# Computing the front of each later layer inside the last batch or chunk of the layer before it

## The chip, the cores and the metric

The program runs on one core of a Trainium2 chip. Its engines are TensorE (PE), VectorE (DVE), ScalarE (ACT), GpSimd (POOL) and SyncE (SP), which here only issues DMAs. The metric is device time in microseconds of one execution. A pair of kernels is compared by several executions of each on the same chip.

## The reference, cut to what matters

x has 16 batches of 256 tokens with 128 features. Four residual layers follow each other, each on the layer norm of x:

```python
x = x + mamba(layernorm(x))        # 16 states per channel, 256 channels, scan over 256 tokens
x = x + experts(layernorm(x))
x = x + attention(layernorm(x))    # 16 heads of 8, weights 1/(eps + distance)^2; it norms and adds its input again
x = x + experts(layernorm(x))      # the same weights as the first experts
```

The expert layer, for one token:

```python
scores = sigmoid(x @ gate_w.T)                       # 16 experts
inds = top_k(scores + expert_bias, 8)
combine = 2.826 * scores[inds] / sum(scores[inds])   # 0 for the others
y = sum_e combine[e] * w_down[e] @ (silu(w_gate[e] @ x) * (w_up[e] @ x))
y = y + shared_down @ (silu(shared_gate @ x) * (shared_up @ x))
```

All 16 experts are computed for all tokens here, and the combine weight of an expert that wasn't chosen is 0.

## The kernel before

**Stages.** x stays in SBUF (`x_sb`) for the whole program. The four layers are four calls, `mamba_layer`, `expert_layer`, `attention_layer`, `expert_layer`, each in a block of its own: all engines meet at the end of a block before any goes on to the next. Inside a block each engine has its own list of instructions, written by hand: a prologue, a first body, a hardware loop of two bodies, last bodies and an epilogue. Engines wait for each other by semaphores (`take` waits and lowers again, `Chain` makes an engine wait for its own last result). No scheduler changes this order.

**Mamba** runs by batch of 256 tokens. A body has 8 steps m (PAIRS); in each, ACT computes the decays (`L498`), POOL the inputs (`L270`), DVE the scan over time (`L643`) and its product with C (`L598`), and PE adds the states up into `m_y_ps` (`add_states`, `L374`). DVE multiplies y by the gate (`gate_y`, `L586`), PE projects out, DVE updates x (`L592`). In the block's epilogue the expert weights are converted from float32 to two float16 halves: ACT makes all the upper halves; POOL the lower halves of the down and router weights (`L312` to `L314`); DVE those of gate and up (`ew_gate_up`) in three pieces (`L666`) of 6, 6 and 5 experts, with `gate_y` and the update of the last batch between them.

**Experts** run by chunk of 512 tokens, 8 chunks. For a chunk, the front is: statistics (DVE `L1005`), norm (POOL `L838`), normalise (DVE `L1015`), transpose (PE `L861`), split into halves `x_hi` (ACT) and `x_lo` (DVE `L1020`), routing products (PE), the sigmoid by tanh (ACT), and `choose` in three parts (DVE `L1029` to `L1043`: eight linked steps from the scores to `e_comb`). PE transposes the combine weights (`L875`), ACT reads them into `e_cT`, SP stores them to DRAM (`mix`, `L805`) and loads them back spread over all partitions (`e_c_bc`, `L810`, four loads of four experts each). Then 17 steps e (16 experts and the shared one): PE computes gate and up in three matmuls each (`L885`) into one of BANKS = 3 pairs of PSUM banks `g`, `u`; ACT applies silu (`L956`), DVE multiplies by the combine weight (`e_cu`, `L1056`) and by the other half (`e_h`, `L1061`), ACT and POOL split h into halves (`L961`, `L845`), and PE multiplies by the down weights (`L892`) three steps later. A bank is free again when `e_h` has been made. The front of chunk q + 1 runs inside the body of chunk q; that of chunk 0 is the block's prologue, where the engines do nothing else, except that PE runs up to the third expert ahead. The last chunk of the layer has no front in it. x is updated at `L1066`.

**Attention** runs by batch, three batches deep. The front of a batch: statistics (DVE `L1407`), norm (POOL `L1207` to `L1213`, seven linked steps), normalise (DVE `L1418`), transpose (PE `L1271`) and projection to q, k, v, gate (PE `L1277`), read with bias (DVE `L1428`), packing and squares (POOL `L1229`), splitting q and k into halves with their norms (DVE `L1439` to `L1447`), 16 transposes (PE `L1286`) and their read (DVE `L1454`). Then 16 heads: scores (PE `L1295`), distances (DVE `L1461`), sqrt, ln and exp (ACT `L1384`, `L1388`, `L1392`), weighing of the values (PE `L1303`), division, gate, output projection, update of x (`L1497`). The prologue of the block zeroes the padded tiles (POOL), computes the front of batch 0, then the statistics and norm of batch 1.

## Time and profile before

| | us |
|---|---|
| three runs | 1593.68, 1592.61, 1593.71 |
| their median | 1593.68 |
| the profiled execution | 1592.62, of which the span is 1590.9 |
| busy PE | 1308.6 (82%) |
| busy DVE | 1273.3 (80%) |
| busy ACT | 1097.2 (69%) |
| busy POOL | 897.1 (56%) |

The shares are means over four stages with different limits: Mamba up to about 534 us, the first expert layer to 843, attention to 1278, the second expert layer to the end. They say nothing about the places where one stage hands over to the next; these are read in the timeline. The clock of TensorE has two levels, 1.2 and 2.4 GHz, and the granted clock of a stretch is given as a share of the upper one; over the whole execution it was 0.887.

### The profile page before, as it was taken

The numbers are of one execution on the slowest core, as the hardware profiler recorded it, in microseconds if no ns is written. First come the engines' busy times: TensorE is split into PE (matmuls) and PEld (weight loads), VectorE is DVE, ScalarE is ACT, GpSimd is POOL, SyncE is SP. The second block draws the span as 40 slices with busy tenths as digits, with TensorE's granted clock in tenths as the row PEclk, the third lists the DMA queues.
The fourth block names the chain that finished last, engine by engine and source line by source line (L and its number), as shares of the span: only waits on it lengthen the run. The fifth ranks groups of instructions, "written<-read, shape, count | busy, mean of one in ns | idle before, by whom it ended". The sixth has DMA issues, their size and how long they took to land. (4 is left out here: it accounts for less than half of the span.)

```text
span 1590.9 us, 21353 instructions
## 1 busy us (share of the span) xinstructions
PE 1308.6 (82%) x6384; PEld 626.4 (39%) x6384; DVE 1273.3 (80%) x2163; ACT 1097.2 (69%) x1578; POOL 897.1 (56%) x1052
## 2 busy tenths in 40 slices
PE   4688888888886499999994777778878569999998
PEld 3344444444442244444441233333333224444443
DVE  2899999999999678878864788888887357877775
ACT  4667767867866255555550899999999935555554
POOL 5898888889877365555554322322321025555555
PEclk8899999999999799999996577867766569999999
DMA  7122122122110132222220000000000022223330
GB/s 239 54 80 81 53 71 88 53 69 91 53 70 37 77 137 108 107 106 106 106 107 0 1 1 0 0 0 0 0 0 1 1 107 114 114 113 126 149 149 35
DMA packets 27923, 111.54 MB, mean 70 GB/s; under 512 B 4049, under 2 KB 9570, under 8 KB 19426
## 3 DMA queue, kind: packets, MB, share of 16 engines
q1 hardware_dynamic: 27010, 110.21, 18.5%
q10 hardware_dynamic: 864, 0.74, 0.1%
q8 instruction: 22, 0.36, 0.1%
q14 instruction: 27, 0.22, 0.0%
HBM read 108.06 MB, written 2.88 MB: 70 GB/s over the span
## 5 line engine op out<-in xcount | busy, mean ns | idle before, releaser
L845 POOL TENSOR_TENSOR e_h_lo<-e_h,e_h_hi 128x512 f16<-128x512 f32 x272 | 314.7, 1157 | 273.3 <-ACT e_h_hi L961 262.2
L270 POOL TENSOR_TENSOR m_h<-m_b_sb,m_dx 128x512 f32<-128x512 f32 x256 | 345.0, 1374 | 49.1 <-POOLq L67 40.4
L498 ACT ACTIVATE m_decay<-m_delta,mw_a_log 128x255 f32<-128x255 f32 x448 | 185.3, 461 | 119.4 <-DVEq L648 119.2
L643 DVE TENSOR_TENSOR_SCAN m_h<-m_decay,m_h 128x1024 f32<-128x1024 f32 x112 | 255.8, 2284 | 13.2 <-DVEq L60 7.5
L1056 DVE TENSOR_TENSOR e_cu<-e_u,e_c_bc 128x512 f32<-128x512 f32 x256 | 175.9, 687 | 108.7 <-PE e_u L885 87.5
L956 ACT ACTIVATE e_g<-e_g 128x512 f32<-128x512 f32 x256 | 149.1, 582 | 162.8 <-PE e_g L885 162.8
L374 PE MATMUL m_y_ps<-m_hc,ident 128*128 128x512 f32 x512 | 250.4, 613 | 0.0
L885 PE MATMUL e_g<-e_x_hi,ew_gate_up 128*128 128x512 f16 x544 | 210.2, 386 | 9.4 <-ACTq L960 9.4
L1461 DVE TENSOR_SCALAR a_d<-a_s 128x512 f32<-128x512 f32 x256 | 170.3, 686 | 56.7 <-PE a_s L1295 36.8
L885 PE MATMUL e_u<-e_x_hi,ew_gate_up 128*128 128x512 f16 x544 | 209.2, 385 | 0.0
L892 PE MATMUL e_y<-e_h_hi,ew_down 128*128 128x512 f16 x544 | 206.9, 381 | 1.6 <-POOL e_h_lo L845 1.6
L961 ACT ACTIVATE e_h_hi<-e_h 128x512 f16<-128x512 f32 x272 | 169.5, 623 | 55.7 <-DVE e_h L1061 54.9
L1061 DVE TENSOR_TENSOR e_h<-e_g,e_cu 128x512 f32<-128x512 f32 x256 | 176.9, 691 | 15.9 <-DVE e_cu L1056 1.1
L598 DVE TENSOR_TENSOR m_hc<-m_h,m_c_ps 128x1024 f32<-128x1024 f32 x128 | 152.8, 1194 | 0.6 <-PE m_c_ps L369 0.6
L1295 PE MATMUL a_s<-a_qkT 32*128 32x256 f16 x512 | 105.6, 341 | 57.7 <-DVE a_d L1461 42.8
L374 PEld LDWEIGHTS m_y_ps<-m_hc,ident 128*128 128x128 f32 x512 | 92.8, 197 | 73.0 <-issue 70.4
L1384 ACT ACTIVATE a_d<-a_d 128x2048 f32<-128x2048 f32 (+1 forms) x48 | 115.7, 2469 | 5.7 <-ACTq L67 5.5
L369 PE MATMUL m_c_ps<-m_bc,m_pick 96*128 96x256 f16 x256 | 49.4, 274 | 83.0 <-DVE m_hc L598 72.4
L1388 ACT ACTIVATE a_d<-a_d,a_near 128x4096 f32<-128x4096 f32 x32 | 116.9, 3701 | 0.2
L1392 ACT ACTIVATE a_d<-a_d 128x2048 f32<-128x2048 f32 x64 | 116.7, 1894 | 0.0
L885 PE MATMUL e_g<-e_x_lo,ew_gate_up 128*128 128x512 f16 x272 | 105.1, 386 | 0.0
L885 PE MATMUL e_u<-e_x_lo,ew_gate_up 128*128 128x512 f16 x272 | 104.6, 385 | 0.0
(190 smaller groups left out, 1999.5 us busy)
## 6 DMA issues: line engine op xcount, KB each, us to landing
e_c_bc<-mix SPq DMA_DIRECT2D x64, 1024.0 KB, 6.8
m_b_sb<-b_rows SPq DMA_DIRECT2D x64, 512.0 KB, 5.4
ew_gate_up<-w_gate_up SPq DMA_DIRECT2D x1, 2176.0 KB, 13.5
out<-x_sb SPq DMA_DIRECT2D x8, 256.0 KB, 2.3
ew_down<-w_down SPq DMA_DIRECT2D x1, 1088.0 KB, 11.5
mw_conv_rows<-w_conv_rows ACTq DMA_DIRECT2D x1, 640.0 KB
mix<-e_cT SPq DMA_DIRECT2D x16, 32.0 KB, 1.6
x_sb<-x SPq DMA_DIRECT2D x1, 256.0 KB, 3.1
```

What stands on the lines that cost most here:

```text
L270: ins = nc.gpsimd.tensor_tensor(h[:, m % 4, :, c], b_sb[:, p, 2 * m:2 * m + 2], dx[:, p, c:c + 1].to_broadcast([P, 2, T]), ALU.mult)
L374: ins = nc.tensor.matmul(y_ps[:], ident[:], hc[:, m % 2, n].rearrange("p c t -> p (c t)"), start=(m == 0 and n == 0), stop=(m == PAIRS - 1 ...
L498: ins = nc.scalar.activation(decay_of(m, p)[:, at + 1:at + T], delta[:, p, c, 1:T], ACT.Exp, scale=neg_a[:, c, 2 * m + n:2 * m + n + 1])
L598: nc.vector.tensor_tensor(hc[:, m % 2], h[:, m % 4], c4, ALU.mult).then_inc(hc_ready, 1)
L643: nc.vector.tensor_tensor_scan(flat, decay_of(m, p)[:], flat, 0.0, ALU.mult, ALU.add).then_inc(scan_chain, 1)
L845: nc.gpsimd.tensor_tensor(h_lo[:, k], h[:, k], h_hi[:, k], ALU.subtract).then_inc(h_lo_ready, 1)
L885: ins = nc.tensor.matmul(ps[bank][:], ew.gate_up[r][:, e, side], a[:, p], start=(n == 0), stop=(n == 2))
L892: ins = nc.tensor.matmul(y_ps[:], ew.down[r][:, e], a[:, place(e)], start=(e == 0 and n == 0), stop=(e == NE and n == 2))
L961: nc.scalar.activation(h_hi[:, place(e)], h[:, place(e)], ACT.Copy).then_inc(h_hi_ready, 1)
L1056: nc.vector.tensor_tensor(cu[:, e % 2], u_ps[bank][:], c_bc[:, e], ALU.mult).then_inc(core_chain, 1)
L1061: nc.vector.tensor_tensor(h[:, place(e)], g_ps[bank][:], cu[:, e % 2], ALU.mult).then_inc(h_ready, 1)
L1461: ins = nc.vector.tensor_scalar(d[:, p, h], s_ps[h % 2][:], -2.0, 0.0, ALU.mult, ALU.max)
```

## The change

The instructions of a front no longer belong to the layer that uses them but to two new classes, `ExpertFront` (tiles and semaphores `ef_...`) and `AttentionFront` (`af_...`), whose tiles live on through several blocks. The layer before calls them at fixed steps of its last body.

**Mamba to experts.** In the last batch: statistics of chunk 0 at m = 0 (DVE), norm at m = 1 (POOL), normalise at m = 2 (DVE), transpose at m = 1 (PE, into the free bank `t1`), upper half at m = 4 (ACT), lower half at m = 5 (DVE), routing at m = 4 (PE), sigmoid at m = 6 (ACT, by exp, so that DVE's `choose` has a reciprocal more), `choose(0)` at m = 7; in the epilogue `choose(1)`, `choose(2)`, transpose, read, store and the load of the first four experts' weights, `ef_c_head`. The other twelve (`e_c_rest`) are loaded by the prologue of the expert layer. ACT's conversions of the weights stand between the decays of the last batch. POOL makes the lower halves of down (all 17) and of gate and up for experts 11 to 16, DVE those for experts 0 to 10 in two pieces.

**Experts to attention.** POOL's zero fills run at the start of the first expert layer. The front of batch 0 runs in that layer's last chunk, on the third pair of banks, so that this chunk has two pairs for its own work instead of three. The norm of batch 1 is what POOL does first in the attention block.

**Attention to experts.** In the last batch: statistics and normalise (DVE, h = 0 and 1), transpose (PE, h = 2), both halves (DVE, h = 3), routing (PE, h = 5), sigmoid between Ln and the exps on ACT, `choose` (DVE, h = 14), transpose (PE, h = 14, ahead of `weigh`), read (DVE, h = 15), store and first load (SP).

The core of the diff:

```diff
@@ mamba_layer: SP, POOL, PE, ACT, DVE
             sp_eng.sem_inc(raw_ready, 1)
+            front.store_mix(sp_eng, 0, mix)
+            front.load_c(sp_eng, 0, 0, mix, None)
...
+                    if m == 1 and last:
+                        front.norm(pool)
+                        lower_router()
...
-                for raw, halves in ew.parts[1:]:
+                for part, own in ((DOWN, slice(0, NE + 1)), (GATE_UP, slice(ON_VECTOR, NE + 1))):
...
+                    if m == 1 and last:
+                        front.transpose_x(pe, t1)
+                    if m == 4 and last:
+                        take(pe, router_lower)
+                        front.route(pe, 0, t1)
...
+                    if last:
+                        if m == 0:
+                            take(act, raw_ready)
+                            upper_weights(ROUTER, 0, NE, router_upper)
+                        if m in (1, 2, 3):
+                            upper_weights(GATE_UP, 6 * m - 6, min(6 * m, NE + 1), upper["dve"] if m == 2 else upper["pool"] if m == 3 else None)
+                        if m == 4:
+                            front.upper_x(act, 0, t1)
+                        if m == 5:
+                            upper_weights(DOWN, 0, NE + 1, upper["pool"])
+                        if m == 6:
+                            front.squash(act, t1, by_exp=True)
...
+                    if m == 0 and last:
+                        front.statistics(dve, 0)
+                    if m == 2 and last:
+                        front.normalise(dve, 0)
+                    if m == 5 and last:
+                        front.lower_x(dve, 0, t1)
+                    if m == 7 and last:
+                        front.choose(dve, 0, by_exp=True)
                     dve.wait_ge(decay_ready, m + 1)
...
+                front.choose(dve, 1)
+                front.choose(dve, 2)
+                gate_y((NB - 1) % 2)
                 take(dve, upper["dve"])
-                for e in range(0, NE + 1, 6):
...
+                lower_weights(0, 6)
+                update(NB - 1)
+                lower_weights(6, ON_VECTOR)
@@ expert_layer
+        def banks(last):
+            return 2 if last and nxt is not None else BANKS
...
+                    if last and nxt is not None:
+                        nxt.pool_step(pool, e)
                     lower(e)
...
+                    if last and nxt is not None:
+                        nxt.tensor_step(pe, e, g_ps[2], u_ps[2])
...
+                    if last and nxt is not None:
+                        nxt.vector_step(dve, e, g_ps[2], u_ps[2])
@@ AttentionFront
+    def pool_step(self, pool, e):
+        if e == 1:
+            self.norm(pool)
+        if e == 4:
+            self.residual(pool, 0)
+        if e == 9:
+            self.pack(pool, 0)
...
+        if e == 4:
+            self.transpose_z(pe, banks[0])
+        if e == 7:
+            self.project(pe, banks)
+        if e == 14:
+            self.transpose_qk(pe, banks)
...
+            self.statistics(dve, 0)
+        if e == 3:
+            self.normalise(dve, 0)
+        if e == 6:
+            self.read_zT(dve, banks[0])
+        if e == 8:
+            self.read_qkvg(dve, 0, banks)
+        if e == 9:
+            self.statistics(dve, 1)
+        if e == 12:
+            self.split_qk(dve, 0)
+        if e == 15:
+            self.read_qkT(dve, 0, banks)
@@ attention_layer
+                if last:
+                    experts.squash(act, t_ps[0], by_exp=True)
...
+                    if last and h == 14:
+                        for part in range(3):
+                            experts.choose(dve, part, by_exp=True)
```

How this moves instructions, engine by engine, at three places. DVE at the end of the last Mamba batch, before:

```order
L643 SCALAR_TENSOR_TENSOR m_h<-m_decay,m_h 128x1024
L598 TENSOR_TENSOR m_hc<-m_h,m_c_ps 128x1024 x2
L666 SCALAR_TENSOR_TENSOR ew_gate_up<-ew_gate_up 128x1536
L586 TENSOR_TENSOR m_yg<-m_y_ps,m_gate 128x512
L666 SCALAR_TENSOR_TENSOR ew_gate_up<-ew_gate_up 128x1536
L592 TENSOR_TENSOR x_sb<-m_t,x_sb 128x256
L666 SCALAR_TENSOR_TENSOR ew_gate_up<-ew_gate_up 128x1280
```

and after, from `choose(0)` at m = 7 to the gate multiply:

```order
L888 TENSOR_SCALAR ef_th<-ef_th 128x64
L889 RECIPROCAL ef_score<-ef_th 128x64
L892 TENSOR_TENSOR ef_sel<-ef_score,ew_bias 128x64
L894 MAX ef_top<-ef_sel 128x8 x4
L690 SCALAR_TENSOR_TENSOR m_h<-m_decay,m_h 128x1024
L637 TENSOR_TENSOR m_hc<-m_h,m_c_ps 128x1024 x2
L898 MATCH_REPLACE ef_left<-ef_top,ef_sel 128x16 x4
L900 SCALAR_TENSOR_TENSOR ef_chosen<-ef_left,ef_score 128x64
L902 TENSOR_REDUCE ef_total<-ef_chosen 128x4
L903 RECIPROCAL ef_total<-ef_total 128x4
L905 SCALAR_TENSOR_TENSOR ef_comb<-ef_chosen,ef_total 128x64
L625 TENSOR_TENSOR m_yg<-m_y_ps,m_gate 128x512
```

Part 0 of `choose` now stands ahead of the last scan (`L690` after, `L643` before), parts 1 and 2 between the last multiply and the gate multiply, where the first piece of conversion stood.

PE from the last chunk of the first expert layer into attention, before (the branches are the end of one block and the start of the next):

```order
L898 MATMUL e_t<-ident,e_yT 128x128 x4
L725 UNCONDITIONAL_BRANCH
L1262 UNCONDITIONAL_BRANCH
L1271 MATMUL a_t<-ident,a_z 128x128 x2
L1277 MATMUL a_t<-aw_qkvg_w,a_zT 128x512 x2
L1286 MATMUL a_t<-ident,a_qk 128x128 x16
L1295 MATMUL a_s<-a_qkT 128x256 x4
```

and after, at the same place:

```order
L1075 MATMUL e_t<-ident,e_yT 128x128 x4
L942 UNCONDITIONAL_BRANCH
L1498 UNCONDITIONAL_BRANCH
L1508 MATMUL a_s<-af_qkT 128x256 x4
L1302 MATMUL a_t<-ident,af_z 128x128 x2
```

The scores of the first head follow the branch directly; the transposes, projections and 16 more transposes of batch 0 are gone from here, and stand between the matmuls of the last chunk.

SP from Mamba into the experts, before:

```order
L212 COMPARE_AND_BRANCH
L103 UNCONDITIONAL_BRANCH
L800 UNCONDITIONAL_BRANCH
L805 DMA mix<-e_cT 16x512
L810 DMA e_c_bc<-mix 128x2048 x4
```

and after:

```order
L215 COMPARE_AND_BRANCH
L928 DMA mix<-ef_cT 16x512
L934 DMA ef_c_head<-mix 128x2048
L103 UNCONDITIONAL_BRANCH
L1004 UNCONDITIONAL_BRANCH
L934 DMA e_c_rest<-mix 128x2048 x3
```

The store and the first load are issued inside the Mamba block, the three other loads in the expert block.

## Rows read from the trace of the kernel before

**Rows 1.** The page's 40 slices of the span: granted TensorE clock in tenths.

```profile
PEclk8899999999999799999996577867766569999999
```

**Rows 2.** Timeline, Mamba to experts: start, us, engine, line, operation, out<-in, [idle before].

```profile
515.64 2.28 DVE L643 TENSOR_TENSOR_SCAN m_h<-m_decay,m_h 128x1024 f32<-128x1024 f32 x1
517.84 1.19 DVE L598 TENSOR_TENSOR m_hc<-m_h,m_c_ps 128x1024 f32<-128x1024 f32 x1
...
526.46 0.69 DVE L586 TENSOR_TENSOR m_yg<-m_y_ps,m_gate 128x512 f32<-128x512 f32 x1 [0.50 <-DVEq L67]
...
533.78 0.87 DVE L1005 BATCH_NORM_STATS2 e_stats<-x_sb 128x6 f32<-128x128 f32 x4 [0.31 <-PEq L103]
...
541.86 0.19 DVE L1029 TENSOR_SCALAR e_score<-e_th 128x64 f32<-128x64 f32 x1 [1.24 <-DVEq L67]
...
544.44 0.23 DVE L1043 SCALAR_TENSOR_TENSOR e_comb<-e_chosen,e_total 128x64 f32<-128x64 f32 x1
...
546.64 0.32 SPq L805 DMA_DIRECT2D mix<-e_cT  x1
...
553.22 0.69 DVE L1056 TENSOR_TENSOR e_cu<-e_u,e_c_bc 128x512 f32<-128x512 f32 x1 [8.56 <-DVEq L67]
...
554.74 0.61 PE L885 MATMUL e_g<-e_x_hi,ew_gate_up 128*128 128x512 f16 x1 [4.54 <-ACTq L960]
```

**Rows 3.** Timeline, last chunk of the first expert layer, DVE and PE, experts 14 to 16.

```profile
833.44 0.69 DVE L1056 TENSOR_TENSOR e_cu<-e_u,e_c_bc 128x512 f32<-128x512 f32 x1 [0.53 <-PE e_u L885]
...
835.38 0.69 DVE L1056 TENSOR_TENSOR e_cu<-e_u,e_c_bc 128x512 f32<-128x512 f32 x1 [0.53 <-PE e_u L885]
...
835.83 0.38 PE L885 MATMUL e_g<-e_x_hi,ew_gate_up 128*128 128x512 f16 x1
...
836.22 0.69 DVE L1061 TENSOR_TENSOR e_h<-e_g,e_cu 128x512 f32<-128x512 f32 x1
```

**Rows 4.** Windows: stretch, us, busy PE, PEld, DVE, ACT, POOL, clock, DMA, GB/s.

```profile
541.00:549.00 8.00, 7.12 (x27) 2.67 (x28) 2.34 (x18) 1.97 (x4) 0.00 (x0) 0.50 0.03 6
555.00:560.00 5.00, 5.00 (x14) 1.85 (x13) 4.63 (x14) 2.73 (x6) 4.19 (x5) 0.54 0.92 390
```

**Rows 5.** Timeline, experts to attention: last update, first scores, ACT's last early wait.

```profile
842.80 0.69 DVE L1066 TENSOR_TENSOR x_sb<-e_t,x_sb 128x512 f32<-128x512 f32 x1 [4.74 <-DVEq L67]
...
866.99 0.61 PE L1295 MATMUL a_s<-a_qkT 32*128 32x256 f16 x4 [0.88 <-PEq L67]
...
887.29 1.91 ACT L1384 ACTIVATE a_d<-a_d 128x2048 f32<-128x2048 f32 x1 [3.79 <-ACTq L67]
```

**Rows 6.** Timeline, attention to experts: last update, transposes of combine weights, expert 3.

```profile
1277.96 0.42 DVE L1497 TENSOR_TENSOR x_sb<-a_u,x_sb 128x256 f32<-128x256 f32 x1 [1.60 <-DVEq L67]
...
1289.59 1.01 PE L875 MATMUL e_t<-ident,e_comb 128*16 128x128 f32 x4 [0.88 <-PEq L67]
...
1299.52 0.61 PE L885 MATMUL e_g<-e_x_hi,ew_gate_up 128*128 128x512 f16 x1 [4.88 <-ACTq L960]
```

**Rows 7.** Instructions of one line: ns min/median/max, first and last start, forms.

```profile
L666 DVE SCALAR_TENSOR_TENSOR ew_gate_up<-ew_gate_up x3: 1474/1914/4675, 524.0 to 532.0; 128x1536 f16<-128x1536 f32 x2, 128x1280 f16<-128x1280 f32 x1
...
L313 POOL TENSOR_SCALAR ew_router<-ew_router x1: 1710/1710/1710, 530.1 to 530.1; 128x16 f32<-128x16 f32 x1
...
L1015 DVE TENSOR_SCALAR e_xn<-x_sb,e_mv,e_nrm x64: 331/338/1282, 536.7 to 1525.8; 128x128 f32 x48, 128x128 f32<-128x128 f32 x16
```

**Rows 8.** Timeline, prices of moved steps: PE's float32 products, POOL's norm, DVE's split.

```profile
516.08 1.88 PE L374 MATMUL m_y_ps<-m_hc,ident 128*128 128x512 f32 x4
...
848.94 0.19 POOL L1207 TENSOR_SCALAR a_nrm<-a_mv 128x2 f32<-128x2 f32 x1 [1.20 <-POOLq L67]
...
851.60 0.20 POOL L1213 TENSOR_TENSOR a_nrm<-a_nrm 128x2 f32<-128x2 f32 x1
...
861.70 0.76 DVE L1439 TENSOR_TENSOR a_qk<-a_qkvg,a_qk 128x256 f16<-128x256 f32 x2 [2.92 <-DVEq L67]
...
863.67 0.44 DVE L1447 TENSOR_TENSOR a_qk<-a_norms,a_qk 128x32 f16<-128x32 f32 x2
```

More of the change, by code:

```diff
@@ L550, in body, with upper_weights @@
                 scanned.end(first, last)
+            def upper_weights(part, start, stop, ready=None):
+                raw, halves = ew.parts[part]
+                ins = nc.scalar.activation(halves[0][:, start:stop], raw[:, start:stop], ACT.Copy, scale=W_SCALE)
+                if ready is not None:
+                    ins.then_inc(ready, 1)
             def epilogue():
-                take(act, raw_ready)
-                for n, (raw, halves) in enumerate(ew.parts):
-                    nc.scalar.activation(halves[0][:], raw[:], ACT.Copy, scale=W_SCALE).then_inc(upper["dve"] if n == 0 else upper["pool"], 1)
+                front.read_c(act, 0, t1)
             batches(act, body, prologue, epilogue)
@@ L724, in expert_layer @@
+def expert_layer(nc, sems, own_sems, layer, front, x_sb, ew, ident, mix, out=None, nxt=None):
     ctx = ExitStack()
@@ L829, in epilogue @@
                     take(sp, used)
[L831 removed]
+            chunks(sp, body, prologue, epilogue)
         @block.gpsimd
         def _(pool):
[L835 to L840 removed]
             def lower(e):
@@ L886, in up @@
                     ins.then_inc(ready, 1)
-                if first and e == 0:
-                    transpose_comb()
             def down(e):
@@ L1046, in hidden @@
-            def hidden(e):
-                bank = e % BANKS
+            def hidden(e, last):
+                bank = e % banks(last)
                 if e < NE and e % GROUP == 0:
-                    take(dve, c_loaded[e // GROUP], 16)
+                    take(dve, front.c_loaded[e // GROUP], 16)
                 dve.wait_ge(u_ready, e + 1)
@@ L1104, in attention_layer @@
+def attention_layer(nc, sems, x_sb, aw, loaded, front, experts, mix, ident):
     ctx = ExitStack()
@@ L1245, in prologue, with body @@
-                pack(0)
-                norm()
-            def body(b, p, core=True, tail=True, heads=True, ahead=True, further=True):
+                front.norm(pool)
+            def body(b, p, core=True, tail=True, heads=True, ahead=True, further=True, last=False):
+                if last:
+                    experts.norm(pool)
                 if ahead:
-                    residual(b + 2)
+                    front.residual(pool, b + 2)
                 if tail:
@@ L1512, in body @@
                     if h == 0 and ahead:
-                        normalise(b + 2)
+                        front.normalise(dve, b + 2)
+                    if last:
+                        if h == 0:
+                            experts.statistics(dve, 0)
+                        if h == 1:
+                            experts.normalise(dve, 0)
+                        if h == 3:
+                            experts.upper_x_on_vector(dve, 0, t_ps[0])
+                            experts.lower_x(dve, 0, t_ps[0])
                     if h == 2 and tail:
@@ L1544, in epilogue, with program @@
                 update(NB - 1)
-            batches(dve, body, prologue, epilogue)
-def program(nc, x, w, out, mix, b_rows, layers=("mamba", "experts", "attention", "experts")):
+            batches(dve, body, lambda: None, epilogue)
+def program(nc, x, w, out, mix, b_rows):
     ctx = ExitStack()
@@ L1565, in program @@
         later += [(dst, src, loaded["experts"]) for dst, src in ew.loads(w)]
-        if "attention" in layers:
-            later += [(dst, src, loaded["attention"]) for dst, src in aw.loads(w)]
+        later += [(dst, src, loaded["attention"]) for dst, src in aw.loads(w)]
         with nc.Block() as block:
@@ L1589, in _ @@
                                             pattern=[[-1, P]], channel_multiplier=1)
-        for n, layer in enumerate(layers):
-            if layer == "mamba":
-                mamba_layer(nc, ctx, x_sb, mw, loaded, later, ew, ident, half, b_rows)
-            if layer == "experts":
-                last = n == len(layers) - 1
-                expert_layer(nc, ctx, expert_sems, n, x_sb, ew, ident, half, mix[n % 2], out.rearrange("b (n p) d -> p (b n) d", p=P) if last else None)
-            if layer == "attention":
-                attention_layer(nc, ctx, x_sb, aw, loaded, ident, ident16, half)
+        with early:
+            mamba_layer(nc, ctx, x_sb, mw, loaded, later, ew, ident, half, b_rows, front, mix[0])
+        with middle:
+            attention = AttentionFront(nc, middle, ctx, x_sb, aw, ident, ident16, half)
+            expert_layer(nc, ctx, expert_sems, 1, front, x_sb, ew, ident, mix[0], nxt=attention)
+            attention_layer(nc, ctx, x_sb, aw, loaded, attention, front, mix[1], ident)
+        expert_layer(nc, ctx, expert_sems, 3, front, x_sb, ew, ident, mix[1], out=out.rearrange("b (n p) d -> p (b n) d", p=P))
 def layout(v):
```

718 lines of the change are left out of this document (388 added, 330 removed).

## Prediction

> **What bounds the kernel now.** The 40-slice view gives the clock of TensorE first: nearly full in the first third (Mamba) and in the two expert layers, 5 to 7 tenths in attention [rows 1]. Each layer has a limit of its own, and the change touches none of them; it touches the three seams between layers. I read those in the timeline.
>
> Seam A, Mamba to experts [rows 2]: in the last batch DVE runs scan and multiply back to back (515.64 to 517.92, then from 517.84), with no idle. The expert layer's first statistics come at 533.78, its combine weights leave for DRAM at 546.64, and the first `e_cu` runs at 553.22 after 8.56 us of idle. PE had filled its three banks and waited 4.54 us more, so expert 3 starts at 554.74. In steady state experts follow each other every 1.94 us (833.44 to 835.38), nine matmuls each [rows 3], so a matmul is 0.215 at full clock and 0.43 at half. The clock rows show half clock from 541 to 549, and again for most of 555 to 560, where PE was full [rows 4]. The second stretch, 554.74 to about 559.4, loses 2.3 us, so expert 3 began in effect at 557.1.
>
> Seam B, experts to attention [rows 5]: x is updated from 842.80 to 843.49, the first score starts at 866.99, and ACT, of which attention is then a chain without gaps, ends its last early wait at 887.29. From 843.49 to 866.99 stands the front of batch 0, one chain: 23.5 us.
>
> Seam C, attention to experts [rows 6]: the last update runs from 1277.96 to 1278.38, expert 3 starts at 1299.52 after the same kind of wait, so with the same 2.3 us lost in effect at 1301.8.
>
> **Part 1, seam A.** Statistics, norm, transposes, routing, choosing, the store and the first quarter of the load leave the seam. They land on a DVE without slack, so their DVE steps cost their full price in the last batch:
> - statistics: 0.87 for four, 0.4 for the aggregates: 1.3 [rows 2].
> - normalise: four instructions, 0.33 each where nothing is in the way and 1.28 in the worst of 64 [rows 7]: 1.3 to 5.1. POOL feeds the scans beside it, and its norm ends just as DVE arrives; the median is the nearest row, one step held up comes on top: 2.2.
> - the subtraction for `x_lo`, one pass over 512 columns: 0.7 [rows 3].
> - choose: eight linked steps took 541.86 to 544.67 [rows 2], 0.35 each. Part 0 has three of them and one new reciprocal, 1.4, and 0.3 for a result that comes through PE and ACT barely in time. Not in the trace: POOL converts the down weights at that moment. Lower bound 0; upper bound 5.7, which is the 4.7 of the conversion row that was held up plus 1.0 for its greater width; I take 1.5, half the way to the gap of 3.2 between the slow and the quick row there [rows 7].
> - choose, parts 1 and 2, the other five steps, 1.8: nothing. DVE waits for y there; a first piece of weight conversion (1.9) and 0.50 of idle fill the place now [rows 2, 7]. If y were early, they would cost 1.8.
>
> Sum 7.4 (4.7 to 14.5). The gate multiply moves from 526.46 to 533.9. Behind it stood 0.7 for itself, conversions of 4.7 and 1.5 and a small update; 0.7 + 1.9 + 0.4 + 1.5 stand there now, as POOL takes the last six experts, 4.3 with their overlaps. DVE ends at 538.2, PE starts expert 0 at 538.5 (a seam is 0.31 [rows 2]). ACT's conversions stand between the decays; I cost them nothing, since no scan in these rows waits for ACT. A piece that overran would delay a scan by as much.
>
> `c_head`: choose ends about when y does, 533.9; from there the 1.97 of 544.67 to 546.64 and the 6.58 of 546.64 to 553.22 [rows 2] give 542.4, about a us after PE's half-clock expert 0 (538.5 + 2.6 = 541.1). The other three quarters go out behind the seam and are wanted at expert 4. Three banks of six matmuls at half clock take 18 x 0.43 = 7.7: expert 3 at 546.2. **Gain 557.1 - 546.2 = 10.9** (4 to 16).
>
> **Part 2, seam B.** PE's share of the front goes onto a PE that is full: two float32 products of 512 columns, 1.9 (four records in one row [rows 8]); two transposes, 0.3, from four at 1.01 at half clock [rows 6]; sixteen transposes of 128 columns, 16/36 of an expert's columns, 0.9: 3.1. DVE's share is larger: statistics twice 0.7, normalise 1.3, zT 0.4, qkvg 1.4, split 2.4 (861.70 to 864.11 [rows 8]), qkT 1.4: 8.3, against an idle of 0.53 in each 1.94 [rows 3]. New is that expert e waits for e-2 instead of e-3. In [rows 3] expert 15's `e_h` ends at 836.91; PE began expert 16 at 835.83 and would begin 17 at 837.77, so two banks leave 0.8 to spare. An extra X in one slot stalls PE by X - 0.5 - 0.8, in two adjacent slots by X - 1.0 - 0.8. Normalise and the old update (1.3 + 0.7): 0.2. qkvg and statistics (1.4 + 0.7): 0.3. Split: 1.1. POOL's norm, 2.9 (848.94 to 851.80 [rows 8]), makes `h_lo` late by 0.2. That is 1.8; where POOL and DVE meet in the split I add 1.0. qkT stands ahead of the last expert and delays the tail by 0.8. The chunk ends 6.7 later (bounds 3.1, all of DVE hidden, and 14, all of it on the path with 2.6 of meetings).
>
> Attention then starts with scores at 843.5 + 6.7 + 0.5 = 850.7. DVE's second step there is the normalise of batch 1, whose norm now starts on POOL only with the block: 2.9 against 1.6 until DVE arrives, so 1.3 more (0 to 2.9), and the waiting DVE holds up its next scores. POOL's zero fills move to the start of the expert layer, where POOL waits for work anyway. **Gain 866.99 - 852.0 = 15.0** (7 to 20).
>
> **Part 3, seam C.** In the last batch DVE, PE and POOL wait for ACT, so the routing hides. ACT gets one small activation, one linked step, 0.35, at full price. PE's transposes of the combine weights, 1.01 at half clock [rows 6], stand between the first and second `weigh`, where PE is the late one: 1.4 in all (0.3 to 3). PE starts at 1278.38 + 1.4 + 0.3 = 1280.1, expert 3 at 1287.8. **Gain 1301.8 - 1287.8 = 14.0** (10 to 17).
>
> **Sum.** 10.9 + 15.0 + 14.0 = 39.9. The profiled execution took 1592.62 (span 1590.9), 1.06 under the median of 1593.68: 1552.7 there, 1553.8 against the median.
>
> **Rivals.**
> 1. *The clock stays full over the seams.* PE's pause shrinks to some 3 us. Then A is limited by `c_head` (542.4 and two passes: expert 3 at 543.9, 2.3 more), C by six fast matmuls per bank (3.8 more), and B's first batch has its products 1.9 faster: 1546. Against: sparse work ran at half clock in [rows 4]. 13%.
> 2. *POOL stops DVE.* `L666` took 4.675 us where another piece took 1.474, and a 16-column POOL instruction beside it 1.710 [rows 7]: one waited out the other. In the last Mamba batch POOL now has two and a half such pieces of conversion beside choose, and in the chunk its packing beside the split. At the upper bounds A loses 7.1 and B 4 to 7 more: 1561 to 1568, so 1564. 17%. The Trainium skill, "SBUF — State Buffer", section "Who interferes with whom", has a rule for it: a DVE instruction with two SBUF inputs and a GpSimd instruction that reads SBUF exclude each other, and the second waits in full. By that rule choose, the conversions and the split are at risk and the scans with their decay in PSUM are free; the slow pair above agrees, and no row here proves the scans' freedom.
> 3. *The fronts are moved but not hidden*, each delaying its host by what it was worth: 1593. Every engine would have to be the late one; at seam C all but ACT wait. 2%.
> 4. *Slower: the clock falls in the two-bank chunk and stays down.* In attention a PE with short waits is held near half clock (the slices of 5 and 6 [rows 1]). If the stalls of the last chunk do the same, and then the first chunks of both expert layers, each us at half clock loses half a us; it turns to a loss from 80 us of half clock beyond those counted, more than two chunks. Against: in a first chunk a half-clock PE is itself the limit, so it has no waits, and [rows 4] shows the clock back within 8 us. 1600. 3%.
>
> **How the numbers follow.** My forecast, 1549 to 1560, has 65%; the rivals 13, 17, 2 and 3. The range reaches into rivals 1 and 2: 1545 to 1565. A measurement of this kernel can tell about 0.2% (3 us) from no change; forecast and rivals 1 and 2 are all faster by that: faster 0.95, same 0.02, slower 0.03.
>
> **What would show it.** The first `e_cu` of each expert layer 4 to 6 us after its block's start instead of 19; the scans of the last Mamba batch spread by some 7 us in all; in the last chunk of the first expert layer PE waits of 1 to 2 us for the release of a bank near experts 11 and 14; the first score within 1 us of the seam. Wrong would be: a scan that waits for a decay or for POOL, `c_head` arriving after PE has filled three banks, or half clock for longer than 10 us after a seam.

## The result

Four executions of each kernel on the same chip: 1593.23 us (median) before, 1555.12 us after, a ratio of 0.9762 (95% interval 0.9749 to 0.9776). The forecast was 1553.8. The profiled execution of after took 1555.15, 37.47 less than the profiled one of before; the last update of x comes 1587.26 - 1549.79 = 37.47 earlier. Two single executions of later kernels lay far outside all others, 2136.27 of `choose_late` and 6807.43 of `warm_gap`; the medians below are over the others.

The shares on the page rise by two points each (PE 84%, DVE 82%, ACT 71%, POOL 58%): about the same work in a span that is 2.4% shorter. The clock in 40 slices has the same shape as before [rows 1], with a mean of 0.900 against 0.887:

```profile
PEclk9799999999999899999998567878776689999999
```

The gain is read at fixed points of the program, from the same instruction in both traces:

| point | before | after | earlier by |
|---|---|---|---|
| first `e_cu`, first expert layer | 553.22 | 546.87 | 6.35 |
| first `e_cu` of its last chunk | 805.80 | 799.43 | 6.37 |
| last update of x in that layer | 842.80 | 841.52 | 1.28 |
| first score of attention | 866.99 | 842.67 | 24.32 |
| end of ACT's early wait | 887.29 | 864.77 | 22.52 |
| last update of x in attention | 1277.96 | 1255.68 | 22.28 |
| first `e_cu`, last expert layer | 1298.00 | 1259.17 | 38.83 |
| second `e_cu` there | 1299.33 | 1261.62 | 37.71 |
| expert 8 of the same chunk | 1313.50 | 1275.99 | 37.51 |

Between the seams the shift is constant to 0.3: the layers themselves run as before. So seam A gave 6.35, seam B 22.28 - 6.37 = 15.9 (after 5.1 paid in the last chunk), seam C 37.51 - 22.28 = 15.2. The forecast had 10.9, 15.0 and 14.0. The sum came out 2.4 from the forecast's 39.9 because A's shortfall of 4.5 was half made up by the other two.

**Seam A after.** DVE in the last Mamba batch and up to the first `e_cu` (timeline: start, us, engine, line, operation, out<-in, [idle before <- releaser]; answers to [rows 2]):

```profile
504.19 0.69 DVE L625 TENSOR_TENSOR m_yg<-m_y_ps,m_gate 128x512 f32<-128x512 f32 x1 [0.80 <-DVEq L67]
504.80 3.01 DVE L838 TENSOR_SCALAR ef_xn<-x_sb,ef_mv,ef_nrm 128x128 f32<-128x128 f32 x4
...
525.21 2.10 DVE L888 TENSOR_SCALAR ef_th<-ef_th 128x64 f32<-128x64 f32 x1
527.35 0.55 DVE L889 RECIPROCAL ef_score<-ef_th 128x64 f32<-128x64 f32 x1
527.94 0.84 DVE L892 TENSOR_TENSOR ef_sel<-ef_score,ew_bias 128x64 f32<-128x64 f32 x1
...
529.44 2.29 DVE L690 TENSOR_TENSOR_SCAN m_h<-m_decay,m_h 128x1024 f32<-128x1024 f32 x1 [0.22 <-DVEq L60]
...
536.28 0.22 DVE L905 SCALAR_TENSOR_TENSOR ef_comb<-ef_chosen,ef_total 128x64 f32<-128x64 f32 x1
539.28 0.69 DVE L625 TENSOR_TENSOR m_yg<-m_y_ps,m_gate 128x512 f32<-128x512 f32 x1 [2.77 <-DVEq L67]
...
546.87 0.69 DVE L1170 TENSOR_TENSOR e_cu<-e_u,ef_c_head 128x512 f32<-128x512 f32 x1 [3.39 <-DVEq L67]
```

`choose(0)` is the four steps from 525.21 (the fourth, `L894`, is not shown); the next scan starts at 529.44, so it cost 4.23. PE and SP over the same time, POOL beside them, and the clock in windows (stretch, us, busy PE, PEld, DVE, ACT, POOL, clock, DMA, GB/s):

```profile
525.66 1.88 PE L391 MATMUL m_y_ps<-m_hc,ident 128*128 128x512 f32 x4
532.99 0.58 PE L386 MATMUL m_c_ps<-m_bc,m_pick 96*128 96x256 f16 x2 [5.44 <-DVE m_hc L637]
533.37 5.76 PE L391 MATMUL m_y_ps<-m_hc,ident 128*128 128x512 f32 x8
538.96 0.60 PE L912 MATMUL m_t<-ident,ef_comb 128*16 128x128 f32 x4
```

```profile
540.38 0.32 SPq L928 DMA_DIRECT2D mix<-ef_cT  x1
```

```profile
522.95 4.32 POOL L331 TENSOR_TENSOR ew_down<-ew_down 128x2176 f16<-128x2176 f32 x1
527.23 1.47 POOL L330 TENSOR_SCALAR ew_gate_up<-ew_gate_up 128x1536 f32<-128x1536 f32 x1
```

```profile
526.00:530.00 4.00, 1.54 (x4) 0.38 (x2) 3.68 (x8) 0.00 (x0) 3.92 (x3) 1.00 0.00 0
530.00:534.00 4.00, 1.01 (x3) 0.68 (x4) 3.23 (x3) 0.00 (x0) 1.88 (x1) 0.61 0.00 0
534.00:538.00 4.00, 4.00 (x6) 1.56 (x5) 2.26 (x13) 0.00 (x0) 0.00 (x0) 0.54 0.00 0
```

Two things meet. `L888`, an instruction on 64 columns that takes 0.20 where POOL is idle, ends at 527.31, just as POOL's `L331` ends (527.27); `L892` ends at 528.78 as POOL's `L330` ends (528.70). And while DVE waits, PE waits 5.44 for it, the clock falls to half, and the eight matmuls that add up the last states take 5.76 instead of 3.60. The combine weights are ready on DVE at 536.50, but their transposes stand on PE behind those matmuls (538.96), so the store goes out at 540.38.

The same chain had run once before in this batch, on a smaller scale. The statistics hold DVE up, PE waits 2.88 for it instead of 1.37, the clock falls (0.57 from 500 to 504, 1.00 in the kernel before), and four matmuls of the add-up take 3.29 where they took 1.88. That is why the gate multiply at 504.19 stands after an idle of 0.80:

```profile
500.37 0.58 PE L386 MATMUL m_c_ps<-m_bc,m_pick 96*128 96x256 f16 x2 [2.88 <-PEq L67]
500.75 3.29 PE L391 MATMUL m_y_ps<-m_hc,ident 128*128 128x512 f32 x4
```

**Seam B after.** The waits of PE among the experts of the last chunk (engine, line, waited for: us in total, times, longest; its tail is left out), the front's largest steps on PE, and the timeline around the seam (answers to [rows 5]):

```profile
PE e_g L1064 <- ACTq L1123: 0.3, 1, 0.3
PE e_g L1302 <- PEq L67: 0.3, 1, 0.3
PE e_g L1317 <- PEq L67: 0.2, 1, 0.2
```

```profile
815.06 1.02 PE L1308 MATMUL e_g<-aw_qkvg_w,af_zT 128*128 128x512 f32 x2
815.92 1.02 PE L1308 MATMUL e_u<-aw_qkvg_w,af_zT 128*128 128x512 f32 x2
...
830.80 0.61 PE L1317 MATMUL e_g<-ident,af_qk 128*128 128x128 f16 x8 [0.18 <-PEq L67]
831.25 0.61 PE L1317 MATMUL e_u<-ident,af_qk 128*128 128x128 f16 x8
```

```profile
841.52 0.69 DVE L1180 TENSOR_TENSOR x_sb<-e_t,x_sb 128x512 f32<-128x512 f32 x1 [4.69 <-DVEq L67]
...
845.64 0.60 DVE L1334 TENSOR_SCALAR af_z<-x_sb,af_mv,af_nrm 128x128 f32<-128x128 f32 x2 [1.67 <-DVEq L67]
```

The single wait for a bank is 0.3 (`L1064`); in the other two PE waits for the front's own normalise and split. From the first `e_cu` to PE's start on the last expert the chunk is 4.5 longer (from 799.43 to 833.96, before from 805.80 to 835.83), and most of that is PE's own work: 1.7 for the projections, 1.2 for the 16 transposes, 0.4 for the two transposes of z. Another 0.6 comes from DVE, which reads q and k ahead of the last `e_h`. At 845.64 DVE has waited 1.67 for the norm of batch 1.

**Seam C after** (answers to [rows 6]):

```profile
1255.68 0.43 DVE L1657 TENSOR_TENSOR x_sb<-a_u,x_sb 128x256 f32<-128x256 f32 x1 [1.47 <-DVEq L67]
1259.17 0.69 DVE L1170 TENSOR_TENSOR e_cu<-e_u,ef_c_head 128x512 f32<-128x512 f32 x1 [3.06 <-PE e_u L1064]
...
1261.62 0.69 DVE L1170 TENSOR_TENSOR e_cu<-e_u,ef_c_head 128x512 f32<-128x512 f32 x1 [1.03 <-PE e_u L1064]
```

Here the weights are there in time, and DVE waits for PE (`<-PE e_u`), which starts at half clock.

### The profile page after: what moved, and what is told of

The parts are those of the page before. It is cut to its first block and busy times, and to the rows that moved or that the text cites. A ratio compares the mean times of both kernels' runs of the same rounds, so it can differ in the third digit from the quotient of the medians.

```text
span 1553.4 us, 21357 instructions
## 1 busy us (share of the span) xinstructions
PE 1301.2 (84%) x6384; PEld 625.0 (40%) x6384; DVE 1278.3 (82%) x2166; ACT 1096.8 (71%) x1578; POOL 900.2 (58%) x1054
## 3 DMA queue, kind: packets, MB, share of 16 engines
HBM read 108.06 MB, written 2.88 MB: 71 GB/s over the span
## 5 line engine op out<-in xcount | busy, mean ns | idle before, releaser
L690 DVE TENSOR_TENSOR_SCAN m_h<-m_decay,m_h 128x1024 f32<-128x1024 f32 x112 | 256.0, 2285 | 13.5 <-DVEq L60 7.7
L391 PE MATMUL m_y_ps<-m_hc,ident 128*128 128x512 f32 x512 | 260.4, 634 | 0.0
L1621 DVE TENSOR_SCALAR a_d<-a_s 128x512 f32<-128x512 f32 x256 | 170.4, 688 | 56.4 <-PE a_s L1508 37.5
L1064 PE MATMUL e_g<-ef_x_hi,ew_gate_up 128*128 128x512 f16 x544 | 207.6, 382 | 3.8 <-PEq L103 2.4
L1064 PE MATMUL e_u<-ef_x_hi,ew_gate_up 128*128 128x512 f16 x544 | 207.8, 382 | 0.0
L1170 DVE TENSOR_TENSOR e_cu<-e_u,e_c_rest 128x512 f32<-128x512 f32 x192 | 132.1, 688 | 61.0 <-PE e_u L1064 56.6
L1508 PE MATMUL a_s<-af_qkT 32*128 32x256 f16 x512 | 103.7, 336 | 62.3 <-DVE a_d L1621 45.1
L1064 PE MATMUL e_u<-ef_x_lo,ew_gate_up 128*128 128x512 f16 x272 | 104.1, 383 | 0.0
L1064 PE MATMUL e_g<-ef_x_lo,ew_gate_up 128*128 128x512 f16 x272 | 103.8, 382 | 0.0
```

What stands on the lines that cost most here:

```text
L391: ins = nc.tensor.matmul(y_ps[:], ident[:], hc[:, m % 2, n].rearrange("p c t -> p (c t)"), start=(m == 0 and n == 0), stop=(m == PAIRS - 1 ...
L690: nc.vector.tensor_tensor_scan(flat, decay_of(m, p)[:], flat, 0.0, ALU.mult, ALU.add).then_inc(scan_chain, 1)
L1064: ins = nc.tensor.matmul(ps[bank][:], ew.gate_up[r][:, e, side], a[:, p], start=(n == 0), stop=(n == 2))
L1621: ins = nc.vector.tensor_scalar(d[:, p, h], s_ps[h % 2][:], -2.0, 0.0, ALU.mult, ALU.max)
```

## Experiments

Every median is set beside after's 1555.12, which was measured once. The runs came in three sets, each on a chip of its own; the kernel before took 1592.59 in the set of `undo_a`, `undo_b`, `undo_c` and `undo_b_two_banks`, 1593.11 in that of `pool_after`, `choose_late`, `warm_gap` and `norm_early`, and 1592.79 in that of the others, against 1593.23 beside after. The first expert layer's first `e_cu` came at 545.25 to 547.99 in five traces whose kernels have the same Mamba code as after. So a difference of 1 us between two medians is not read; the differences inside the traces are.

### Each seam undone alone

`undo_a` puts the front of chunk 0 back into the prologue of the first expert layer, with the conversions as they were:

```diff
+            def prologue():
+                if own:
+                    front.statistics(dve, 0)
+                    front.normalise(dve, 0)
+                    front.lower_x(dve, 0, t_ps)
+                    for part in range(3):
+                        front.choose(dve, part)
```

> Only seam A is undone: the front of the first expert layer's chunk 0 is back in that layer's prologue, the weight conversions back in Mamba's epilogue; seams B and C stay as changed (median 1555.1). Theory 1, from the shifts of the first combine-weight multiplies in the two traces (6.4 us all through the first expert layer): about 1561.5. Rival, the split of the prediction (10.9): about 1566.0. If the gains of the seams overlap, less than either.

Measured 1564.81 (1564.24 to 1566.00), 9.7 more than after, between the two theories. The trace shows why: the last scan of Mamba starts as in the kernel before (519.1 and 519.0), but then DVE's normalise takes 4.00 where it took 1.11. What is different from before is that POOL's zero fills, moved by the change to this block, run beside it:

```profile
536.82 4.00 DVE L799 TENSOR_SCALAR ef_xn<-x_sb,ef_mv,ef_nrm 128x128 f32<-128x128 f32 x4 [1.64 <-DVEq L797]
```

```profile
536.62 1.80 POOL L1244 MEMSET af_qk<- 128x2048 f16 x1
538.37 1.80 POOL L1245 MEMSET af_v<- 128x2048 f32 x1
```

So a further run took the fills out of its way, behind `choose`:

```diff
+                    take(pool, chosen)
                     nxt.zeros(pool)
...
                     for part in range(3):
                         front.choose(dve, part)
+                    dve.sem_inc(chosen, 1)
```

> As the run with seam A undone, but POOL zeroes attention's tiles only when DVE has made the combine weights, so not beside DVE's normalise. Theory (DVE's four instructions took 4.00 instead of 1.11 because POOL was zeroing beside them): 2.9 less than that run, about 1561.9, which makes seam A worth 6.4 to 6.8 net of it. Rival (the collision is not the cause, the seam is worth 9.7): 1564.8 again.

Measured 1561.37 (1559.59 to 1562.54); the normalise is back at its price:

```profile
537.09 1.11 DVE L799 TENSOR_SCALAR ef_xn<-x_sb,ef_mv,ef_nrm 128x128 f32<-128x128 f32 x4 [1.64 <-DVEq L797]
```

Seam A is worth 1561.37 - 1555.12 = 6.25 by the medians and 553.41 - 546.87 = 6.54 by the first `e_cu`, as the traces of before and after say (6.35), and not the 10.9 of the forecast. The 4.00 was the collision.

`undo_b` takes the three calls `nxt.pool_step`, `tensor_step` and `vector_step` out of the last chunk, gives it three pairs of banks and puts the same steps into the prologue of attention:

```diff
-            return 2 if last and nxt is not None else BANKS
+            return BANKS
```

> Only seam B is undone: the front of attention's batch 0 is back in the attention block's prologue and the last chunk of the first expert layer has three pairs of banks again; the zero fills stay at the start of the expert layer. Theory 1, from the shifts in the traces (6.4 before the seam, 22.3 to 22.5 in attention: 16.0): about 1571.1. The prediction's split (15.0): 1570.1.

Measured 1568.08 (1566.46 to 1568.43): 13.0, less than both numbers. Inside the trace the seam costs 12.35 (from the first `e_cu` of the last chunk to the last update of x in attention 800.24 to 1268.84, in after 799.43 to 1255.68), against 15.9 between before and after. The difference of 3.6 is close to what the zero fills cost there; this run leaves them at the start of the expert layer. In the kernel before, DVE stood still for them at the start of attention:

```profile
847.98 0.49 DVE L1407 BATCH_NORM_STATS2 a_stats<-x_sb 128x6 f32<-128x128 f32 x2 [4.10 <-POOLq L1200]
```

and in this run it did not:

```profile
837.24 0.69 DVE L1176 TENSOR_TENSOR x_sb<-e_t,x_sb 128x512 f32<-128x512 f32 x1 [4.74 <-DVEq L67]
...
838.27 0.49 DVE L1317 BATCH_NORM_STATS2 af_stats<-x_sb 128x6 f32<-128x128 f32 x2
```

So some 4 of the 23.5 that stood at seam B were not the front at all, but five memsets on POOL; they were moved by the same change. No run moved the fills alone.

`undo_c` does the same for the last expert layer. 

> Only seam C is undone: the front of the last expert layer's chunk 0 is back in its prologue. Theory 1, from the shifts (22.4 at the end of attention, 37.5 in the last layer: 15.1): about 1570.2. The prediction's split (14.0): 1569.1.

Measured 1569.39 (1569.14 to 1569.64): 14.3, between the two numbers. Inside its trace the seam costs 15.25, as theory 1 has it: from the last update of x in attention to the ninth `e_cu` of the next layer it takes 1254.47 to 1290.03, in after 1255.68 to 1275.99. The execution as a whole is only 14.06 longer, because its Mamba layer came out ahead (first `e_cu` at 545.25, 1.62 before after's). The three seams undone one by one give 6.2 + 13.0 + 14.3 = 33.5 by the medians and 6.5 + 12.4 + 15.3 = 34.2 inside the traces. What is missing from the 37.5 between the two profiled executions is 4.0 and 3.3; the wait for the zero fills was 4.1. With medians that scatter by about 1 us the account closes to that much, and no better.

### What two pairs of banks cost alone

As `undo_b`, but the last chunk keeps two pairs (the line above stays as in after). 

> As the run with seam B undone, but the last chunk of the first expert layer uses two pairs of banks and has no front beside it: what two pairs cost alone. Theory: nothing, since a release came 0.8 us before it was wanted in the rows of before: within 0.5 us of the run with seam B undone. Rival, the stalls that the prediction counted for two pairs (1.8 and 1.0) come from the pairs and not from the extra DVE steps: 1.8 to 2.8 us more.

Measured 1566.87 (1566.62 to 1569.29), no more than `undo_b`. From the first to the sixteenth `e_cu` of that chunk `undo_b` takes 829.81 - 800.24, and this run:

```profile
798.51 0.69 DVE L1166 TENSOR_TENSOR e_cu<-e_u,ef_c_head 128x512 f32<-128x512 f32 x1 [1.20 <-PE e_u L1062]
...
828.08 0.69 DVE L1166 TENSOR_TENSOR e_cu<-e_u,e_c_rest 128x512 f32<-128x512 f32 x1 [0.53 <-PE e_u L1062]
```

29.57 in both. Where no front stands beside it, the third pair was free.

### Why seam A fell short: POOL beside choose, and the clock

`pool_after` lets POOL begin its conversions only behind `choose(0)`:

```diff
                 take(pool, upper["pool"], 2)
+                take(pool, scored)
...
                         front.choose(dve, 0, by_exp=True)
+                        dve.sem_inc(scored, 1)
```

> The changed kernel, but POOL begins its weight conversions only when DVE has done part 0 of choose. Theory 1 (in the last Mamba batch DVE's small instructions wait for POOL's conversions: 2.10 us for one that takes 0.20 elsewhere): part 0 of choose falls from 4.2 to about 1.6, PE idles 2.8 instead of 5.4 and keeps its clock, the first combine-weight multiply comes 3 to 3.5 earlier, the program takes about 1552. Rival (choose is long by itself, with exp and reciprocal on the way): choose stays above 4, the program stays at 1555 or loses by POOL's later end.

Measured 1553.18 (1552.87 to 1553.54). Part 0 of `choose` took 1.8 to the next scan instead of 4.2, and its first step:

```profile
524.59 0.18 DVE L890 TENSOR_SCALAR ef_th<-ef_th 128x64 f32<-128x64 f32 x1
```

That decides for theory 1: the steps wait for POOL. Two things came out otherwise than expected. PE's pause shrank to 3.02, but the clock fell all the same, and the add-up took 4.92, not 3.60. And the first `e_cu` came 3.0 earlier (543.83), but the whole run gained only 1.9, because the collision came back on what now stood beside POOL. DVE's conversion took 3.06 instead of 1.75 and put off the end of the block; PE then stood still for 3.58 ahead of the experts (2.39 in after) and began them at half clock, so that the second `e_cu` waited 1.14 for it:

```profile
535.98 3.06 DVE L717 SCALAR_TENSOR_TENSOR ew_gate_up<-ew_gate_up 128x1536 f16<-128x1536 f32 x1
...
546.39 0.69 DVE L1172 TENSOR_TENSOR e_cu<-e_u,ef_c_head 128x512 f32<-128x512 f32 x1 [1.14 <-PE e_u L1066]
```

```profile
541.08 0.58 PE L1066 MATMUL e_g<-ef_x_hi,ew_gate_up 128*128 128x512 f16 x1 [3.58 <-PEq L103]
```

`choose_late` puts the same part behind the last multiply, where PE already has all it needs:

```diff
-                    if m == 7 and last:
-                        front.choose(dve, 0, by_exp=True)
...
                 multiply(PAIRS - 1)
+                front.choose(dve, 0, by_exp=True)
                 front.choose(dve, 1)
```

> The changed kernel, but part 0 of choose stands after the last multiply of Mamba instead of before the last scan, so PE gets the last products 4.2 earlier and has no pause. Theory 1: the add-up runs at full clock and lies beside choose; the three parts of choose end near 535 instead of 536.5, the combine weights reach PE at once; first multiply 3 to 4 earlier: about 1551.5. Rival (the first multiply depends only on when choose ends, whatever PE does): 1 to 1.5 earlier: about 1554.

Measured 1551.07 (1550.50 to 1552.37), 4.0 less than after. The add-up ran at full clock, the first step still waited for POOL (1.62) but beside PE's work, and the first `e_cu` came 3.7 earlier, 2.1 ahead of the earliest of the five traces named above:

```profile
528.75 3.60 PE L391 MATMUL m_y_ps<-m_hc,ident 128*128 128x512 f32 x8
```

```profile
530.09 1.62 DVE L887 TENSOR_SCALAR ef_th<-ef_th 128x64 f32<-128x64 f32 x1
...
543.16 0.69 DVE L1169 TENSOR_TENSOR e_cu<-e_u,ef_c_head 128x512 f32<-128x512 f32 x1 [4.04 <-DVEq L67]
```

To tell the clock from the place of `choose`, `warm_gap` was to fill PE's pause with matmuls that nobody reads:

```diff
+                    if m == 6 and last:
+                        pe.wait_ge(t2_free, 1)
+                        for _ in range(10):
+                            nc.tensor.matmul(t2[:], ident[:], front.xn[:].rearrange("p a d -> p (a d)"), start=True, stop=True)
```

> The changed kernel, with ten additional matmuls on PE (their result is not used) in the pause of 5.4 us while DVE works on choose, so that the clock isn't lowered there. Theory 1: the eight matmuls that add up the last states take 3.6 instead of 5.8, the transposes of the combine weights behind them come 2.2 earlier, and so do the store, the load and the first multiply: about 1553. Rival (the clock there costs nothing): 1555.

A miss: measured 1564.33 (1561.42 to 1564.66). The place was wrong. PE waits at the head of m = 6 for the very product that DVE delays (5.43), so the matmuls came after the pause and delayed the second half of the last add-up:

```profile
536.56 9.10 PE L453 MATMUL m_t<-ef_xn,ident 128*128 128x512 f32 x20
```

With five of them (the trace shows each as two records), and `m == 5` for `m == 6`, they lie in the pause. 

> The changed kernel with five additional float32 matmuls on PE (their result is not used), this time queued behind the sixth pair of add-ups, so that they run in the pause of 5.4 us itself. Theory 1: the clock stays up, the eight matmuls that add up the last states take 3.6 instead of 5.8, and the store of the combine weights and the first multiply come 2.2 earlier: about 1553. Rival (the half clock there costs nothing, the load sets the time): 1555.

Measured 1552.63 (1551.93 to 1553.89), 2.5 less than after, with `choose` as slow as there (2.09 for its first step):

```profile
527.18 4.46 PE L453 MATMUL m_t<-ef_xn,ident 128*128 128x512 f32 x10
532.79 0.51 PE L386 MATMUL m_c_ps<-m_bc,m_pick 96*128 96x256 f16 x2 [1.15 <-DVE m_hc L641]
533.13 3.60 PE L391 MATMUL m_y_ps<-m_hc,ident 128*128 128x512 f32 x8
```

The granted clock from 530 to 538 is 1.00, where after has 0.61 and 0.54; the add-up takes 3.60, and from the end of `choose` to the store it takes 1.75 (536.23 to 537.98) instead of 3.88, and of 3.32 to 3.99 in the five traces named above. The first `e_cu` comes at 544.93, 1.94 earlier, though only 0.3 ahead of the earliest of the five. So about 2 of the 4.5 that seam A lacks are the clock that fell in the pause. The rest of the 2.5 is not the edit's: in this trace another 1.1 came at seam C, which it does not touch, and 0.4 was lost in between.

### What seams B and C still cost

`norm_early` takes the norm of batch 1 from the start of the attention block and lets POOL make it while it waits for DVE in the last chunk:

```diff
         if e == 9:
             self.pack(pool, 0)
+        if e == 13:
+            self.norm(pool)
```

> The changed kernel, but POOL computes the norm of attention's batch 1 at expert 13 of the last chunk, where it waits for DVE, instead of first in the attention block. Theory: the wait of DVE at 845.64 (1.67 us) and PE's pause of 3.1 go, ACT's first sqrt comes 1.3 to 1.7 earlier: about 1553.6. Rival (the half clock of the first batch sets ACT's start, or POOL's extra steps hold up the last experts by as much): 1555.

Measured 1553.37 (1552.62 to 1555.05). In its trace the last layer is 0.14 ahead of after although the first one was 1.06 behind: 1.2 gained between them. DVE's normalise follows the first distance without a wait:

```profile
844.32 0.69 DVE L1620 TENSOR_SCALAR a_d<-a_s 128x512 f32<-128x512 f32 x1 [0.68 <-PE a_s L1507]
844.93 0.59 DVE L1334 TENSOR_SCALAR af_z<-x_sb,af_mv,af_nrm 128x128 f32<-128x128 f32 x2
```

`warm_c` fills PE's pauses in the tail of attention with float16 matmuls of 512 columns that nobody reads, `warm(n)` with n of them:

```diff
                 weigh(HG - 1, 1)
+                warm(4)
                 transpose_av()
+                warm(8)
                 transpose_o()
+                warm(3)
                 project_out()
+                warm(4)
```

> The changed kernel with 19 additional float16 matmuls on PE (their result is not used) in its pauses of the last attention batch's tail (1249 to 1256.4), so that the last expert layer starts at full clock instead of half. Theory: its first two multiplies come 1.3 and 2.3 earlier, from then on DVE sets the pace: about 1552.8. Rival (the matmuls stand in the way of the tail, or the clock falls all the same): 1555 or more.

Measured 1552.41 (1551.89 to 1553.63). The clock stays at 1.00 from 1254 to 1258, where after has 0.63 and 0.50:

```profile
1254.00:1256.00 2.00, 1.65 (x9) 0.85 (x9) 0.45 (x2) 0.02 (x1) 0.00 (x0) 1.00 0.00 0
1256.00:1258.00 2.00, 1.98 (x10) 0.94 (x11) 0.49 (x1) 1.84 (x2) 0.00 (x0) 1.00 0.55 127
```

```profile
1257.51 0.69 DVE L1170 TENSOR_TENSOR e_cu<-e_u,ef_c_head 128x512 f32<-128x512 f32 x1 [1.97 <-PE e_u L1064]
...
1258.85 0.68 DVE L1170 TENSOR_TENSOR e_cu<-e_u,ef_c_head 128x512 f32<-128x512 f32 x1
```

From the first `e_cu` on DVE sets the pace. The trace was 0.56 ahead of after at the last update of x and 2.79 ahead behind the seam: 2.2, as worked out. The tail itself was not delayed but got shorter: at DVE's second read of the weighed values, which no added matmul could yet reach, the trace was 0.19 ahead, so 0.4 of the 0.56 came in the tail.

`all3` joins `choose_late`, `norm_early` and `warm_c`. 

> Three edits of the changed kernel together: part 0 of choose behind the last multiply, the norm of attention's batch 1 at expert 13, and PE kept busy in the tail of attention. If the three places are independent, the gains add: 3.4 + 1.2 to 1.7 + 2.3: about 1548. Rival (the second is hidden as soon as the first or third is there): 1550.

Measured 1547.10 (1546.71 to 1547.83), a ratio of 0.9714 (0.9701 to 0.9727) to the kernel before: 8.0 less than after. The single gains were 4.0 (the expectation counts 3.4), 1.8 and 2.7, 8.5 in all, so they add to within 0.5, and this version beats both kernels.

## Why the prediction held, and where it did not

- **The total** (1553.8 against 1555.12) and the sign were right: the layers between the seams did not change, and a sum over three seams was the right form. That the total came within 1.3 is partly luck: seam A fell short by 4.5, and B and C, which gave 2.1 more than forecast, made up for half of it.
- **Seam A, the step that failed:** `c_head` at 542.4. The first `e_cu` came at 546.87, and the gain was 6.35 instead of 10.9. Two terms of DVE were too small, and one of PE was missing. DVE's steps were put at 7.4. The last scan moved from 518.95 to 529.44, and 0.32 of that was there before the batch. The other 10.2 are 1.20 for the statistics (1.3 priced), 0.33 at the first scan, 3.82 for the normalise with the wait ahead of it (2.2 priced), 0.60 for `x_lo` (0.7 priced) and 4.23 for `choose(0)` (3.2 priced). The 1.5 set aside for POOL beside `choose` was 2.4 by the run that moved POOL (4.2 against 1.8); it had been taken from a gap of 3.2 between rows of different width, 1536 and 1280 columns, which is 2.8 between rows of the same width. The term that was missing altogether is the one of PE: an extra wait on DVE was a pause on PE, the clock fell in the pause, and the add-up behind it, through which the combine weights' transposes had to pass, took 2.2 more. The prediction took 1.97 from `choose` to the store, from a place where PE was idle; it became 540.38 - 536.50 = 3.9. So `choose` ended 2.6 later than the forecast's 533.9, the store took 1.9 more, and the load 0.1 less: the 4.5.
- **Seam A, a wrong model with a harmless result:** the half clock of the first experts (2.3) was counted as a loss of the kernel before. The `e_cu` of the first four experts follow each other in the same rhythm in both traces (553.22, 554.56, 557.07, 558.37 and 546.87, 548.26, 550.79, 552.09), set by DVE. The seam ends at the first `e_cu`, not at expert 3 of PE. Seam C was counted in the same way.
- **Seam B:** 15.0 forecast, 15.9 measured. The chunk ended 5.1 later, not 6.7. PE's share was 3.3 (3.1 priced) and the read of q and k 0.6 (0.8 priced). Of the 2.8 for two-bank stalls and meetings in the split 0.8 came as waits of PE (0.3, 0.3 and 0.2), and only one of these was for a bank; the waits of 1 to 2 us near experts 11 and 14 that the prediction named as a sign did not come, and without the front two pairs cost nothing. DVE's steps did meet POOL there: the normalise took 3.0 (1.1 in the kernel before), and the first step of the split 1.10 (0.76). Apart from those waits this was hidden. The late norm was 1.67 (1.3 priced), and worth 1.2 when it was taken away. The zero fills were inside the 23.5 of the chain, so the sum was right, but the prediction's sentence that they go where POOL waits anyway misses that they had held DVE up by 4.10.
- **Seam C:** 14.0 forecast, 15.2 measured. Of the 1.4 set aside for a later tail only some 0.2 came: ACT's squash took 0.20, and the transposes before `weigh` held nothing up. The half clock at the start costs 2.2, as the run with PE kept busy shows.
- **Rivals.** The first (full clock over the seams) did not come by itself; made by hand at seam C, it is worth 2.2 there, not the 3.8 that this rival gave it, because DVE and not PE's expert 3 sets the end of the seam. The second (POOL stops DVE) is what happens in each collision shown here, at 0.6 to 2.9 us a piece; in the changed kernel `choose(0)` and A's normalise lay on the path. The rule named there in the Trainium skill, "SBUF — State Buffer", section "Who interferes with whom", agrees with the traces on the scans: with their decay in PSUM they took 2.28 to 2.29 beside POOL's conversions. The first scan of the batch, whose decay lies in SBUF (`m_decay_head`), took 2.60 beside a product of POOL (2.28 before, where it started ahead of that product). The same section of the Trainium skill says that a `tensor_scalar` can hold both ports and then excludes GpSimd altogether; the normalise of 4.00 beside memsets, which read nothing, agrees, and the prediction had weighed only the half of the rule on two inputs. The third and fourth rivals (nothing hidden; the clock down for longer) did not come: after the seams the clock was back at full within 10 us at A and C (1.00 from 550 to 554 and from 1262 to 1264). At B it stayed at 0.50 from 842 to 854, as it had before the change from 850 on; the first batch of attention runs mostly at half clock in both kernels.

## What to carry to other kernels

When a front is moved into another stage, price not only the engine that receives it but also the one that waits for that engine: a pause of 5 us on TensorE cost another 2 us through the clock, and everything queued behind it. Put small linked steps where the next consumer already has its data (behind the last multiply instead of before the last scan), and ask what GpSimd does in that microsecond, since a 64-column step can wait 2 us for the end of a conversion. Last, measure each seam at the first instruction that follows a wait and stays shifted to the end of the stage; the shift between stages is then an account that closes.

## What was unexpected about the hardware

- A VectorE `TENSOR_SCALAR` with one tensor input waited for GpSimd: 2.10 instead of 0.18 beside a conversion, 4.00 instead of 1.11 (four of them) beside two memsets. In the same place `RECIPROCAL` took 0.55, as it does at seam C with GpSimd idle.
- Additional float16 matmuls in the pauses of TensorE's tail kept the granted clock at 1.00 and cost nothing that the trace shows; 19 of them were worth 2.2 us at seam C and 0.4 in the tail, and five float32 ones at seam A 1.9.
- The same Mamba code ended up to 2.7 us apart in the traces of kernels that differ only behind it. Between the earliest (`undo_c`) and the latest (`norm_early`), 1.0 was there before the last batch, 0.5 came up to the last scan, 0.7 in the add-up (5.21 and 5.89) and 0.5 between the issue of the first load and the first `e_cu`. What sets these was not tried.
